# Reordering the opening of an adaLN attention and ternary feed-forward kernel

## What is computed

```python
ada = (timestep_embed @ ada_w + ada_b)[:, None, :]
shift1, scale1, gate1, shift2, scale2, gate2 = jnp.split(ada, 6, axis=-1)
x1 = _ln(x) * (1.0 + scale1) + shift1
qkv = (x1 @ qkv_w + qkv_b).reshape(Bc, Tc, 3, H, DH)
attn = softmax(einsum('bthd,bshd->bhts', q, k) * scale)
x = x + gate1 * (attn_out @ out_w + out_b)
x2 = _ln(x) * (1.0 + scale2) + shift2
x = x + gate2 * (gelu(x2 @ ffn_w1 + ffn_b1) @ ffn_w2 + ffn_b2)
out = x_in + bit_ffn(x)      # RMS norm, 8 bit activations, ternary weights
```

## Time and profile before

| | |
|---|---|
| median of 3 runs | 339.4 us (339.18 to 339.67) |
| profiled execution, its own time | 339.61 us |
| its span | 337.8 us |
| TensorE (PE) busy | 330.1 us, 98% of the span |
| VectorE (DVE) busy | 213.7 us, 63% |
| ScalarE (ACT) busy | 182.1 us, 54% |
| GpSimd (POOL) busy | 123.2 us, 36% |

### The profile page before, as it was taken

The page is one execution under the profiler, slowest core; times in us unless marked ns, Lnnn a source line. Parts: engine busy times, 40 slices in busy tenths (PEclk is TensorE's granted clock), DMA queues, the critical chain, the costliest instruction groups (busy, mean ns, idle before and its releaser), DMA issues.

```text
span 337.8 us, 9812 instructions
## 1 busy us (share of the span) xinstructions
PE 330.1 (98%) x4195; PEld 299.4 (89%) x4195; DVE 213.7 (63%) x420; ACT 182.1 (54%) x352; POOL 123.2 (36%) x112
## 2 busy tenths in 40 slices
PE   8999999999999999999999999999999999999886
PEld 8889989899998989899898999789898889998665
DVE  3646966815859943505267236679474789885896
ACT  2654654554426365356433826478535576638694
POOL 2373505000934762555311512133520223305681
PEclk9999999999999999999999999999999999999999
DMA  7984930400045451110020000100010200200001
GB/s 246 369 272 169 308 128 2 156 3 2 2 141 174 158 157 34 64 33 2 2 61 6 3 26 7 55 12 2 2 62 2 64 3 2 65 0 2 31 2 62
DMA packets 20834, 24.41 MB, mean 72 GB/s; under 512 B 1780, under 2 KB 18328, under 8 KB 20792
## 3 DMA queue, kind: packets, MB, share of 16 engines
q1 hardware_dynamic: 20416, 23.50, 21.5%
q10 hardware_dynamic: 376, 0.30, 0.3%
HBM read 22.68 MB, written 1.11 MB: 70 GB/s over the span
## 4 chain that ended last, share of the span: by engine, by line
PE 87%; DVE 6%; ACT 4%; issue 1%; POOL 0%; DVEq 0%; ACTq 0%
PE proj_banks L559 39%; PE out_bank L559 15%; PE att_banks L652 8%; PE wide_banks L559 4%; PE turn_bank L559 3%; PE proj_banks L622 3%; PE wide_banks L843 2%; PE att_banks L559 2%; PE att_banks L887 1%; PE wide_banks L652 1%; ACT work L1768 1%; PE att_banks L843 1%; PE wide_banks L726 1%; ACT L1627 1%; DVE hamax L1400 1%
## 5 line engine op out<-in xcount | busy, mean ns | idle before, releaser
L1634 ACT ACTIVATE q_t<-proj_banks,bias_cols 128x256 f32<-128x256 f32 x64 | 30.5, 477 | 53.9 <-PE proj_banks L559 53.9
L559 PE MATMUL proj_banks<-x_hi,w_hi 128*128 128x256 f32 x252 | 52.8, 291 | 0.0
L559 PE MATMUL proj_banks<-x_lo,w_hi 128*128 128x256 f32 x252 | 50.7, 283 | 0.0
L559 PE MATMUL proj_banks<-x_hi,w_lo 128*128 128x256 f32 x252 | 50.7, 283 | 0.0
L1226 DVE TENSOR_TENSOR v_sb<-proj_banks,bv_row 128x512 f32<-128x512 f32 x32 | 21.8, 685 | 32.3 <-PE wide_banks L652 30.9
L559 PEld LDWEIGHTS proj_banks<-x_hi,w_hi 128*128 128x128 f32 x252 | 39.6, 191 | 1.5 <-issue 0.4
L559 PEld LDWEIGHTS proj_banks<-x_hi,w_lo 128*128 128x128 f32 x252 | 39.2, 191 | 0.0
L559 PEld LDWEIGHTS proj_banks<-x_lo,w_hi 128*128 128x128 f32 x252 | 39.1, 191 | 0.0
L652 PEld LDWEIGHTS att_banks<-probs_t,v_sb 32*128 32x128 f32 x512 | 29.8, 186 | 5.5 <-issue 5.4
L652 PE MATMUL att_banks<-probs_t,v_sb 32*128 32x32 f32 x512 | 31.6, 272 | 0.0
L1634 ACT ACTIVATE k_t<-proj_banks,bias_cols 128x256 f32<-128x256 f32 x64 | 30.2, 471 | 0.0
(11 more groups left out here) (313 smaller groups left out, 790.1 us busy)
## 6 DMA issues: line engine op xcount, KB each, us to landing
stage<-in_L_cond_qkv_w SPq DMA_DIRECT2D x16, 256.0 KB, 4.1
gate<-gate_rows_scratch SPq DMA_DIRECT2D x48, 64.0 KB, 2.5
stage<-in_L_cond_qkv_w SPq DMA_DIRECT2D x4, 512.0 KB, 5.3
stage<-in_L_cond_out_w SPq DMA_DIRECT2D x4, 512.0 KB, 4.4
work<-in_L_ffn_w SPq DMA_DIRECT2D x2, 1024.0 KB, 9.2
xin<-in_x SPq DMA_DIRECT2D x7, 256.0 KB, 4.0
bv_row<-in_L_cond_qkv_b SPq DMA_DIRECT2D x4, 256.0 KB, 5.3
work<-in_L_cond_ada_w SPq DMA_DIRECT2D x1, 1024.0 KB, 9.2
```

Of the source, the lines that this page charges most:

```text
L559: mm = pe.matmul(dst, l, r, start=start and i == 0, stop=stop and i == len(seq) - 1)
L1634: act.activation(dst[:, h, :], proj_bank[h % 2][:, s * QT:(s + 1) * QT], ACT.Identity, bias=bias_cols[:, c:c + 1]).then_inc(qk_kept, 1)
```

## The change

Four things change, all before or beside the first projection.

1. `ADA_COPIES` goes from 4 to 2: the scale and shift matmuls of the opening stream 64 columns in place of 128.
2. On TensorE the shift column 0 no longer stands ahead of `x_turn(0)`. One filler matmul takes its place, the two shift columns follow the token transposes, and the filler behind them grows from 3 to 5 matmuls.
3. ScalarE in place of VectorE copies `cond_t` and `bias_cols` out of the transposes, ahead of its first weight rounding. VectorE starts with the token statistics.
4. The addition of epsilon moves from GpSimd (`x_rstd`) to VectorE (`x_stats`), for all four quarters.

```diff
-    ADA_COPIES = 4
+    ADA_COPIES = 2
...
             pe.transpose(att_bank[0][:, 0:NBIAS], bias_rows, ident[0:NBIAS, 0:NBIAS]).then_inc(turned0, 1)
-            ada_cols(out_bank, 0, ada1_in, (0,), ADA_COPIES, last=False)
+            keep_running(1, of=filler)
             x_turn(0)
-            ada_cols(out_bank, 0, ada1_in, (1,), ADA_COPIES)
-            keep_running(3, of=filler)
+            ada_cols(out_bank, 0, ada1_in, range(KD), ADA_COPIES)
+            keep_running(5, of=filler)
             opening_qk()
...
                     dve.bn_aggr(mv[:, t, :], bn[:, t, :]).then_inc(var_ready, 1)
+                dve.wait_ge(var_ready, 2 * i + 2)
+                dve.tensor_scalar(var_eps[:, 2 * i:2 * i + 2], mv[:, 2 * i:2 * i + 2, 1], LN_EPS, None,
+                                  ALU.add).then_inc(eps_added, 1)
...
-            dve.wait_ge(turned0, 1)
-            dve.tensor_copy(cond_t[:, :, :].rearrange("p k b -> p (k b)"),
-                            proj_bank[0][:, 0:KD * NB]).then_inc(cols_made, 1)
             x_stats(0)
             x_norm(0)
-            dve.wait_ge(turned0, 2)
-            dve.tensor_copy(bias_cols[:, :], att_bank[0][:, 0:NBIAS]).then_inc(cols_made, 1)
             dve.wait_ge(cols_made, 2)
             opening_x()
...
             load_table(ACT.Exp)
+            act.wait_ge(turned0, 1)
+            act.copy(cond_t[:, :, :].rearrange("p k b -> p (k b)"), proj_bank[0][:, 0:KD * NB]).then_inc(cols_made, 1)
+            act.wait_ge(turned0, 2)
+            act.copy(bias_cols[:, :], att_bank[0][:, 0:NBIAS]).then_inc(cols_made, 1)
             high_qk(0, 0)
...
             def x_rstd(i):
-                pool.wait_ge(var_ready, 2 * i + 2)
-                pool.tensor_scalar(var_eps[:, 2 * i:2 * i + 2], mv[:, 2 * i:2 * i + 2, 1], LN_EPS, None,
-                                   ALU.add).then_inc(eps_added, 1)
                 pool.wait_ge(eps_added, i + 1)
                 inv_sqrt(rstd[:, 2 * i:2 * i + 2], var_eps[:, 2 * i:2 * i + 2], rstd_ready)
```

## The result

The change made the kernel slower: 341.06 us in the median of 22 executions (338.93 to 342.55) against 339.5 of the kernel before (339.11 to 340.07); the ratio is 1.0049, with a 95% interval of 1.0034 to 1.0063. The forecast was 339.4, within 338.8 to 340.9; the measured median lies 0.16 above that range.

A forecast was written before the change was run, and what follows sets the result against it. TensorE was taken to set the pace behind the opening, so L589's start decides; the shift columns' +0.16 met VectorE slack, giving 0.0 on the 337.8 us span and a median of 339.4 us, range 338.8 to 340.9.

The forecast's parts named there:

- What bounds the kernel: From 12 to 80 us TensorE alone sets the pace; a shift of L589's start is carried to the end.
- Everything to the bias transpose at 6.96 stays: TensorE's opening: unchanged until 6.96 us, then fillers, transposes and shift records 0.11 apart; last shift record ends at 8.75.
- the sum: Opening to L589: shift columns +0.16 against VectorE's slack, multiply 7.96, L589 at 9.78, so 0.0; chance 0.47.
- the later clock: Opening on TensorE: half the streamed columns keep 1.2 GHz beyond 7.0 us; +1.5, or +2.5 with slow filler; chance 0.20.
- TensorE is as gapless as before, and its weight loads fill the stretch: TensorE between 5.26 and 6.96 us: argument against a clock that rises later; no size of its own.
- The low clock's spacing: Scale records on TensorE before 7 us: at 64 columns still 0.21 us apart, set by the weight load; no gain.
- the rival with faster records: Eight scale records at the low clock 0.11 apart in place of 0.21: L589 at 8.97, -0.8 us, 338.6; chance 0.08.
- tokens ready: Opening on VectorE: normalised tokens ready at 6.46, about 0.6 earlier, a gain hidden behind TensorE's queue.
- ScalarE's copies: Opening: each copy out of the transposes takes 0.27 by interpolation; nothing, at most 0.05 on the multiply.
- epsilon: The addition moved to VectorE takes 0.15 by the nearest row, 0.27 at most.
- Quarters 1 to 3: Later quarters: VectorE gets 0.15 to 0.27 three times, GpSimd loses 0.22 three times; covered, uncovered it would be 0.25.
- The filler ahead of L589: End of the opening on TensorE: ten filler records through at 9.76, up to 0.05 if they hang over.

The follow-up runs named there:

- narrow filler: Kernel before, with only the three constant filler matmuls between condition transposes and scale columns streaming 64 columns in place of 128: 340.58 us, ratio 1.0036.
- the statistics first: Kernel before with ScalarE's two copies, VectorE starting with token statistics and epsilon on VectorE, but four copies and TensorE's old order: 339.45 us, ratio 1.0003.
- full shift columns: Changed kernel with four copies for the shift columns and two for the scale columns: 341.02 us, ratio 1.0029.

## Why the prediction was wrong

**What bounds the kernel** was right: the loss is made before L589 and carried to the end. L589 starts 1.85 later, the span is 1.5 longer. 0.10 of the difference is the first record of L589, whose successor follows after 0.32 where TensorE comes from a wait (before) and after 0.22 where it does not. Another 0.18 comes back soon behind it: between the L559 records at 12.81 and 13.47 of before lie 0.66 us, between the same records of the changed kernel (14.55 and 15.03) 0.48.

**The step that failed** is "Everything to the bias transpose at 6.96 stays. Then two filler records at 7.05 and 7.21", with all that follows spaced at 0.11. It took the clock's rise at about 7.0 from the trace of before as fixed, while the change halved what was streamed ahead of it. In the changed kernel's three traces the rise came at about 11 (once) and 13 us (twice), and L589 started at 11.63 and 12.19 in place of 9.78. With the rise where the sum had it, the sum holds to 0.07 us (scale columns at four copies). With two copies 5 executions of 22 are as short as that; none of them was traced.

**The rival** of the later clock had the mechanism: +1.5 for a low clock until the add, measured 341.07 - 339.61 = +1.46; +2.5 with all the filler slow, L589 at 12.3, measured 342.19 - 339.61 = +2.58, L589 at 12.19. That both prices are met so closely is in part luck. For the first the sum had L589 right behind the add, at 11.29; it started 0.34 later, behind filler that was half slow, and some of that came back behind it. For the second the sum left out that L589's own first records would be slow. Its chance, 0.20, was what was wrong, and with it the upper end of the range. "TensorE is as gapless as before, and its weight loads fill the stretch" was held against it; with the narrow filler both held and the rise still came later.

**The low clock's spacing** at 64 and 32 columns was right at 0.21, so the rival with faster records falls. The Trainium skill's gap that goes with the columns (TensorE: Matmul & The Clock Gate, "Back-to-back issue gap") is given for isolated matmuls, and does not hold for these records with a weight load each: 0.21 at 128, 64 and 32 columns. Its rule that the low clock is the default and activity releases it (Part 1) agrees with the profiles, in which the records are 0.21 apart first and 0.11 later; what these runs show in addition is that fewer streamed columns put the rise off while the busy share of the profile stayed the same.

**The small terms** were right or generous: tokens ready at 6.53 (6.46), ScalarE's copies 0.19 and 0.21 (0.27), epsilon 0.17 (0.15 to 0.27), except for quarter 1, where it took 1.53 (last section). Quarters 1 to 3 cost nothing that shows: with four copies, epsilon on VectorE is within the interval.

**The filler ahead of L589** was priced at up to 0.05. That is right with an early clock. With a late one L589 starts 0.48 (middle level) and 1.04 (upper level) after the add, a second loss hanging on the first.

What stays open: why the clock of one and the same kernel rises at 11 us in one execution and at 13 in another, though their profiles are alike to the digit until then. The traces tell only when.

The moment varies with four copies too. Up to 4.6 us TensorE's records in the trace of the statistics first are those of the kernel before, yet the pace changes at about 4.8 there and at 7.0 before; the other traces with four copies have it between 6.6 and 7.3. The short execution of the kernel before with two copies had it at 5.2, ahead of the narrow records. If the short executions with two copies and with one are such early ones, the narrow scale records could not touch them, and one copy need not do worse than two. That fits the counts and was not shown.

How many columns would be enough to be sure of an early rise was not settled either: with four copies one of 12 and one of 11 executions of two kernels still lay at 340.6.

## What to carry to other kernels

A matmul that only repeats its columns side by side need not be waste while TensorE is still at its low clock. In this kernel the weight load set the pace at 0.21 us a record, so up to 128 columns the extra ones were free, while halving them delayed the rise in 17 of 22 executions and cost 1.5 to 2.6 us in those traced. Look for the clock in the distance between the starts of equal matmuls, not in the granted clock of the page or in busy shares. And before a time of the trace is taken as fixed, ask whether the change touches what it depends on; a median of levels more than 1 us apart should be read as a count of executions on each.

## What the runs showed that had not been expected

The time of one program falls on levels, 1.2 and 1.9 us apart for the changed kernel, rather than around a mean. In its three traces a level goes with the moment at which TensorE's records draw together: about 11 us for 341.1, about 13 us for 342.2. Another kernel has other levels: with the rise at 9.3 us the narrow filler gave 340.58 and the full shift columns 340.75. With one copy the middle level was absent and half of the executions were as short as before; that so few columns still left six of twelve short was not expected.

VectorE's addition of epsilon for quarter 1, two elements in each partition, took 1.53 us in the changed kernel, where the other three took 0.17. GpSimd was subtracting weights beside it (2.41 us from 14.10), and both end within 0.02 us:

```profile
14.72 0.25 DVE L1113 BATCH_NORM_AGGREGATE mv<-bn 128x2 f32<-128x6 f32 x2
15.00 1.53 DVE L1115 TENSOR_SCALAR var_eps<-mv 128x2 f32<-128x2 f32 x1
```

VectorE stood idle for 0.82 us behind it anyway, waiting for GpSimd, so it cost nothing here; what held it was not tested. In every other trace with epsilon on VectorE the longest of the four additions takes 1.50 to 1.53 too.
